# Relative-position values in one attention layer: four queries' columns side by side, all heads and batches moving, and a 32x32 block turn on VectorE

## The chip, the cores and the metric

The program runs on one core of a Trainium2 chip. The metric is the device time of one execution in microseconds (us), as the median of three runs. Lower is better. Everything said of the hardware below is read from one profiled execution of the kernel before the change.

## The reference

The program is a decoder of twelve layers over 8 batches (B) of 128 tokens with 128 channels. The change touches one of them, `l2_attn`: attention with 16 heads of 8 channels and with relative-position embeddings, both for the keys and for the values. Cut to what matters:

```
q, k, v = x @ Wq.T + bq, x @ Wk.T + bk, x @ Wv.T + bv        # (B, T, H*D), B=8, T=128, H=16, D=8
idx = clip(i - j, -128, 128) + 128                           # query i, key j
score1 = einsum('bhqd,bhkd->bhqk', qh, kh)
s2 = einsum('bhqd,qkd->qbhk', qh, rel_k_emb[idx]).reshape(T, H, B, T).transpose(2, 1, 0, 3)
attn = softmax((score1 + s2) / sqrt(D))
w1 = einsum('bhqk,bhkd->bhqd', attn, vh)
se = attn.reshape(B * H, T, T).transpose(1, 0, 2)
w2 = einsum('qnk,qkd->qnd', se, rel_v_emb[idx])              # a table of its own for every query
w2 = w2.reshape(T, H, B, D).transpose(2, 1, 0, 3)            # read back as (head, batch), not (batch, head)
out = (w1 + w2) merged over heads @ Wo.T + bo
```

The change concerns `w2`. For each of the 128 queries there is a table of 128 keys by 8 channels, and it is multiplied with that query's attention weights of all 128 pairs of batch and head. The reference flattens the pairs as (batch, head) and reads them back as (head, batch), so the result of one pair is added to the output of another.

## The kernel before, in words

`layer_l2_attn` (L2400) is one block of the program, with a barrier before and behind it. Each engine runs its own list of instructions in order and waits on semaphores. Its parts, in order of time:

- Projections, and the relative scores: 128 matmuls of L2497, one for each query.
- The attention loop, 16 steps. TensorE makes scores (L508, L2506), VectorE takes the maximum and subtracts it (L584, L590), TensorE turns them (L524), ScalarE takes the exponential into `sm.prob` (L625). `sm.prob` holds, for each of the 128 key partitions, 128 rows (one for each head and batch) of 128 queries (4 bytes each, so one query's value stands 512 bytes from the next row's). `pe_values` (L535) multiplies values with the exponentials: stationary 9 columns (8 channels and a column of ones, which gives the sum of the exponentials), moving 128 neighbouring queries, four matmuls in turn into the partitions 0, 32, 64 and 96 of bank 6. ScalarE copies that bank out (L634), `pe_back` (L543) turns it back into bank 7, and `dve_norm` takes the reciprocal of the ninth column (L597) and multiplies (L599).
- The relative values. For each query q the stationary operand is `relv[:, q, :]` (9 columns, the ninth is ones again), and the moving one is a quarter of the exponentials of that query: 32 rows of `sm.prob`, each one value. Four such matmuls fill the partitions 32i to 32i+8 of a bank, 16 queries a bank, eight rounds for the eight banks (L2539). After each round ScalarE (L2596, even rounds) or VectorE (L2639, odd rounds) copies the bank to `oR`.
- The tail, a batch at a time: four transposes from `oR` to a bank (L2549), reciprocal of the ninth column (L2647), multiplication (L2652), GpSimd adds the result to the attention output (L2462), TensorE turns the sum (L548, `pe_turn_out`), ScalarE copies it (L630, `act_outT`), TensorE projects with Wo (L553, `pe_project`), and VectorE adds it to the residual (L606, `dve_add`).

Then comes the block of `l2_xattn`, which begins with layer norm on VectorE (L421 and on), projections of the context on TensorE (L674, L677) and transposes (L453). The weights of a layer are loaded by a DMA one layer ahead. The banks are eight PSUM tensors of their own.

The two matmuls that the prediction compares, L535 and L2539:

```python
                v = self.nc.tensor.matmul(self.core.ps[6][32 * i:32 * i + 9, j * P:(j + 1) * P],
                                          self.vaug[:, b, 4 * j + i, :], self.prob_of(n)[:, i, :],
                                          start=True, stop=True)
...
                        m = nc.tensor.matmul(
                            ps[r][32 * i:32 * i + 9, 32 * t:32 * t + 32].rearrange("p (b j) -> p b j", b=B),
                            relv[:, q, :], read_by[:, i % 2, i // 2, :, :, q], start=True, stop=True)
```

Of the kernel before, what the change touches and what calls it, by code (L numbers as in the profile page):

```python
# [24 lines left out]
P = 128  # L25

B = 8
# [430 lines left out]
class SmallHeads:  # L458
# [10 lines left out]
    def __init__(self, core, c, wo, more=None, o=None):  # L469
# [9 lines left out]
        self.oT, self.inv, self.o2 = m.take(BANK), m.take(2, 16), m.take(2, P)  # L479
# [4 lines left out]

    def prob_of(self, n):

        return self.prob[:, n % 4, :, :]

# [105 lines left out]
    def dve_norm(self, dve, b, bank):  # L594
        dve.wait_ge(self.back.sem, self.back.at(b))
        o = self.core.ps[bank][:, :].rearrange("p (h d) -> p h d", d=32)
        self.nc.vector.reciprocal(self.inv[:, b % 2, :], o[:, :, 8]).then_inc(self.inverse.sem, self.inverse.up())  # L597
        dve.wait_ge(self.inverse.sem, self.inverse.at(b))
        self.nc.vector.tensor_tensor(self.o_of(b), o[:, :, 0:8],  # L599
                                     self.inv[:, b % 2, :].unsqueeze(2).broadcast_to([P, 16, 8]), ALU.mult) \  # L600
            .then_inc(self.normed.sem, self.normed.up())
# [1785 lines left out]
class RelativeHeads(SmallHeads):  # L2387
# [7 lines left out]

    def prob_of(self, n):
# [3 lines left out]
def layer_l2_attn(core, tag, w):  # L2400
# [12 lines left out]
    oR = qm.rearrange("p i t -> p (i t)").rearrange("p (b j t) -> p b j t", b=B, j=4)  # L2413
    part, part_inv = w.take(2 * 16, 8).rearrange("p (u h) d -> p u h d", u=2), w.take(2, 16)
    made_of = sm.prob.rearrange("p (b h) q -> p b h q", b=B)
    read_by = sm.prob.rearrange("p (y s m z) q -> p y z s m q", y=2, s=8, z=2)
# [11 lines left out]

    def made_in(r, n):
# [5 lines left out]
     rel_made, rel_out_act, rel_out_dve, x_biased, relv_made, relv_act, relv_dve, relv_back,  # L2435
     relv_inverse, relv_normed, relv_summed) = (
        core.count(n) for n in ("ones_set", "x_out", "queries_made", "keys_made", "values_made", "masked_out",
                                "queries_out", "keys_read", "keys_out", "values_out", "rel_made", "rel_out_act",
                                "rel_out_dve", "x_biased", "relv_made", "relv_act", "relv_dve", "relv_back",
                                "relv_inverse", "relv_normed", "relv_summed"))  # L2440
    half = lambda h: slice(h * BANK, h * BANK + BANK)
    with nc.Block(tag, no_gpsimd_drain=True) as block:

        @block.gpsimd
        def _(pool):
# [20 lines left out]
        def _(pe):  # L2466
# [43 lines left out]
            for p in range(-2, sm.STEPS + 2):  # L2510
# [11 lines left out]
                if p % 2 and p >= 3:  # L2522
                    b = (p - 3) // 2
                    pe.wait_ge(sm.outs.sem, sm.outs.at(b))
                    if b > 0:
                        pe.wait_ge(sm.normed.sem, sm.normed.at(b - 1))
                    sm.pe_back(pe, b, 7)
# [5 lines left out]
            for r in range(ROUNDS):  # L2533
                if r == 7:
                    pe.wait_ge(sm.normed.sem, sm.normed.at(B - 1))
                for t in range(TURN):
                    q = r * TURN + t
                    for i in range(4):
                        m = nc.tensor.matmul(  # L2539
                            ps[r][32 * i:32 * i + 9, 32 * t:32 * t + 32].rearrange("p (b j) -> p b j", b=B),  # L2540
                            relv[:, q, :], read_by[:, i % 2, i // 2, :, :, q], start=True, stop=True)
                m.then_inc(relv_made.sem, relv_made.up())
            for step in range(B + 2):
                if step < B:
                    if step == 0:
                        pe.wait_ge(relv_act.sem, relv_act.at(3))
                        pe.wait_ge(relv_dve.sem, relv_dve.at(3))
                    for j in range(4):
                        t = nc.tensor.transpose(ps[step][:, j * P:(j + 1) * P], oR[:, step, j, :], core.ident[:, :])  # L2549
                    t.then_inc(relv_back.sem, relv_back.up())  # L2550
                if 1 <= step <= B:
                    pe.wait_ge(relv_summed.sem, relv_summed.at(step - 1))
                    sm.pe_turn_out(pe, step - 1, step - 1)
                if step >= 2:
                    sm.pe_project(pe, step - 2, step - 2)

        @block.scalar
        def _(act):
# [35 lines left out]
            for r in range(0, ROUNDS, 2):  # L2594
                act.wait_ge(relv_made.sem, relv_made.at(r))
                nc.scalar.copy(oR[:, :, :, r * TURN:(r + 1) * TURN],  # L2596
                               ps[r][:, :].rearrange("p (t b j) -> p b j t", t=TURN, b=B)) \
                    .then_inc(relv_act.sem, relv_act.up())
# [4 lines left out]
        def _(dve):  # L2603
# [33 lines left out]
            for r in range(1, ROUNDS, 2):  # L2637
                dve.wait_ge(relv_made.sem, relv_made.at(r))
                nc.vector.tensor_copy(oR[:, :, :, r * TURN:(r + 1) * TURN],  # L2639
                                      ps[r][:, :].rearrange("p (t b j) -> p b j t", t=TURN, b=B)) \  # L2640
                    .then_inc(relv_dve.sem, relv_dve.up())
            for step in range(B + 2):
                if step < B:
                    b = step
                    dve.wait_ge(relv_back.sem, relv_back.at(b))
# [1371 lines left out]
```

## Time and profile before

| | us |
|---|---|
| median of the three runs shown | 1376.2 |
| lowest and highest of them | 1375.03, 1377.79 |
| span of the profiled execution, first to last instruction | 1375.6 |
| `l2_attn`, relative values (L2539), first start to the last copy out | 903.44 to 932.69 |
| `l2_attn`, tail, to the end of the last residual addition | 932.8 to 943.42 |

Times below are counted from the start of the span. No time of the profiled execution as a whole is given apart from its span; the span lies inside the range of the three runs, 0.6 us under their median. A matmul on float32 operands stands as two records (passes) in the trace, each with a weight load of its own; a transpose stands as one. PE is TensorE, PEld its weight loads, DVE VectorE, ACT ScalarE, POOL GpSimd. PEclk is the granted TensorE clock: 1.00 is 2.4 GHz, 0.50 is 1.2 GHz. The end of a matmul record is modelled, and matmuls overlap, so the time that one takes in a row of many is told by the distance of starts, not by its duration.

### The profile page before, as it was taken

The page shows a single profiled execution, that of the slowest core. Times are in us where ns is not written, and L with a number is a line of the kernel's source. Part 1 is how long each engine was busy: PE and PEld are TensorE (multiplying, and loading weights), DVE is VectorE, ACT ScalarE, POOL GpSimd, SP SyncE. Part 2 cuts the span into 40 slices and gives each one's busy share as a digit, 9 for nine tenths or more (in the row PEclk, how much of TensorE's full clock was granted, in tenths as well). Part 3 has the DMA queues.
Part 4 walks back from the last instruction along what each step waited for, and adds up shares of the span by engine and source line. Part 5 has one row for each costly group of instructions (what it writes and reads, how often), then busy time and mean ns, then how long its engine had stood idle before and what let it go on. Part 6 is the DMA issues. An engine that isn't in the chain of part 4 may idle for free. (4 is left out here: it accounts for less than half of the span.)

```text
span 1375.6 us, 24268 instructions
## 1 busy us (share of the span) xinstructions
PE 1217.7 (89%) x9574; PEld 879.5 (64%) x9574; DVE 701.2 (51%) x2149; ACT 534.1 (39%) x1186; POOL 441.7 (32%) x521
## 2 busy tenths in 40 slices
PE   6999898999868785998798789998989999978997
PEld 5868676788723352665466487795657775556676
DVE  5555543444478335674576466626842125754512
ACT  5534242444355432354345372213433323343232
POOL 7959320000155415672675240003000002031314
PEclk9999999999956587999899999999989998988899
DMA  5000312322091000000000000000020100000412
GB/s 163 1 4 1 142 58 75 95 62 63 21 298 42 1 1 33 1 1 0 1 1 1 9 1 1 1 4 2 1 84 31 47 16 14 1 4 1 140 48 51
DMA packets 51632, 52.42 MB, mean 38 GB/s; under 512 B 19552, under 2 KB 42336, under 8 KB 50496
## 3 DMA queue, kind: packets, MB, share of 16 engines
q1 hardware_dynamic: 50496, 48.77, 11.3%
q0 software_dynamic: 1024, 2.10, 0.7%
q8 instruction: 77, 1.26, 0.4%
q14 instruction: 35, 0.29, 0.1%
HBM read 43.65 MB, written 7.21 MB: 37 GB/s over the span
## 5 line engine op out<-in xcount | busy, mean ns | idle before, releaser
L625 ACT ACTIVATE scratch<-bank 128x512 f32<-128x512 f32 x96 | 52.4, 594 | 87.8 <-PE bank L524 87.8
L584 DVE TENSOR_REDUCE scratch<-bank 128x4 f32<-128x512 f32 x96 | 63.1, 686 | 32.7 <-PE bank L2506 19.5
L447 POOL TENSOR_TENSOR ln_rstd<-ln_ve,ln_half 128x4 f32<-128x4 f32 x28 | 28.7, 1025 | 157.7 <-DVE ln_ve L426 157.6
L2770 POOL TENSOR_TENSOR scratch<-scratch 128x16 f32<-128x16 f32 x16 | 51.7, 3230 | 50.1 <-DVE scratch L3112 50.1
L1126 ACT ACTIVATE scratch<-bank 128x512 f32<-128x512 f32 x64 | 38.2, 597 | 67.8 <-PE bank L1085 67.8
L1095 PEld LDWEIGHTS bank<-scratch 128*128 128x128 f32 x512 | 59.5, 192 | 7.2 <-issue 7.2
L1145 DVE SCALAR_TENSOR_TENSOR x_res<-bank,scratch,x_res 128x128 f32<-128x128 f32 x64 | 18.0, 344 | 88.0 <-PE bank L1095 88.0
L590 DVE TENSOR_TENSOR scratch<-bank,scratch 128x512 f32<-128x512 f32 x96 | 61.4, 681 | 0.0
L1085 PE MATMUL bank<-xnT,scratch 128*128 128x512 f32 x128 | 60.1, 615 | 0.0
L1095 PE MATMUL bank<-scratch 128*128 128x128 f32 x512 | 59.6, 275 | 0.0
L524 PEld LDWEIGHTS bank<-ident,scratch 128*128 128x128 f32 x384 | 42.5, 143 | 22.6 <-DVE scratch L590 15.9
L524 PE MATMUL bank<-ident,scratch 128*128 128x128 f32 x384 | 53.4, 282 | 3.6 <-DVE scratch L590 3.6
L508 PE MATMUL bank<-scratch 32*128 32x512 f32 x192 | 53.3, 635 | 0.8 <-issue 0.8
L2799 PE MATMUL bank<-weights,xnT 128*128 128x512 f32 x64 | 39.5, 714 | 14.5 <-DVE scratch L3082 14.2
L1903 POOL TENSOR_TENSOR x_res<-x_res,scratch 128x256 f32<-128x256 f32 x4 | 2.9, 725 | 141.8 <-ACT scratch L2048 141.8
L2462 POOL TENSOR_TENSOR weights<-weights 128x128 f32<-128x128 f32 x8 | 3.7, 457 | 131.2 <-DVE weights L2652 131.2
L3314 POOL TENSOR_TENSOR scratch<-scratch 128x1024 f32<-128x1024 f32 (+5 forms) x48 | 42.9, 894 | 3.8
L1305 PEld LDWEIGHTS bank<-scratch 128*128 128x128 f32 (+1 forms) x352 | 40.6, 187 | 3.8 <-issue 2.9
L128 PE MATMUL bank<-ident 128*128 128x512 f32 x46 | 31.7, 828 | 12.8 <-PEq L3609 8.3
L3309 POOL TENSOR_TENSOR scratch<-scratch 128x2048 f32<-128x2048 f32 x8 | 36.2, 4525 | 17.8 <-DVE weights L1616 17.3
L2975 ACT ACTIVATE scratch<-bank 128x512 f32<-128x512 f32 x32 | 19.1, 597 | 58.3 <-PE bank L2799 58.3
L1305 PE MATMUL bank<-scratch 128*128 128x128 f32 (+1 forms) x352 | 41.5, 275 | 0.0
(570 smaller groups left out, 3087.3 us busy)
## 6 DMA issues: line engine op xcount, KB each, us to landing
scratch<-conv_kernels SPq DMA_DIRECT2D x8, 1024.0 KB, 11.1
scratch<-e_l_ffn_w SPq DMA_DIRECT2D x20, 256.0 KB, 2.9
scratch<-e_l_ffn_w SPq DMA_DIRECT2D x4, 1024.0 KB, 14.5
values<-scratch SPq DMA_DIRECT2D x8, 512.0 KB, 2.6
scratch<-values SPq DMA_DIRECT2D x8, 512.0 KB, 4.3
weights<-w_l_ffn SPq DMA_DIRECT2D x1, 3698.0 KB, 11.5
scratch<-e_l_ffn_w SPq DMA_DIRECT2D x4, 768.0 KB, 9.5
weights<-w_l_attn SPq DMA_DIRECT2D x1, 2560.5 KB, 8.6
```

Source lines behind the costliest of these rows:

```text
L508: s = self.nc.tensor.matmul(self.by_head(self.core.ps[n % 4][:, :]), self.qT[rows, b * P:(b + 1) * P], self.km[rows, :, b * P:(b + 1) * P] ...
L524: t = self.nc.tensor.transpose(self.core.ps[4 + n % 2][:, i * P:(i + 1) * P], self.shift[:, n % 4, i * P:(i + 1) * P], self.core.ident[:, :])
L584: self.nc.vector.tensor_reduce(self.top[:, n % 4, :], self.by_head(self.core.ps[n % 4][:, :]), AX_X, ALU.max, negate=True).then_inc(self.t ...
L590: self.nc.vector.tensor_tensor(self.by_head(self.shift[:, n % 4, :]), self.by_head(self.core.ps[n % 4][:, :]), self.top[:, n % 4, :].unsqu ...
L625: self.nc.scalar.activation(self.prob_of(n), self.by_head(self.core.ps[4 + n % 2][:, :]), ACT.Exp, scale=scale) \
L1085: nc.tensor.matmul(ps[UP_BANKS[i]][:, :], wa[e % 2][:, i * P:(i + 1) * P], core.xnT[:, half(h)], start=True, stop=True).then_inc(up_made.s ...
L1095: mm = nc.tensor.matmul(ps[Y_BANKS[u % 3]][:, t * P:(t + 1) * P], hT[h][:, i, t * P:(t + 1) * P], wb[e % 2][:, i, :], start=(i == 0), stop ...
L1126: nc.scalar.activation(hT[u % 2][:, i, :], ps[UP_BANKS[i]][:, :], act_func) \
L1305: mm = nc.tensor.matmul(ps[Y_BANKS[j % 3]][0:n, t:t + P], hT[j % 2][:, i, t:t + n], wb[:, e, i, :], start=(i == 0), stop=(i == HC - 1))
L2770: nc.gpsimd.tensor_tensor(rn, ss, power, ALU.pow).then_inc(rooted.sem, rooted.up())
L2799: nc.tensor.matmul(ps[QK_BANKS[n]][:, :], core.xnT[:, b * P:(b + 1) * P], wqkv[d][:, n * BANK:(n + 1) * BANK], start=True, stop=True).then ...
L3314: link(tt(out, prod[:, :, 0:h], prod[:, :, h:2 * h], ALU.add))
```

## The change

The relative values are made by one matmul for each query, not four: stationary `relv[:, q, :]`, now 8 columns (no ones), and moving all 128 rows of `sm.prob` for that query. Four matmuls in turn, for the queries m, 32+m, 64+m and 96+m, go to the partitions 0, 32, 64 and 96 of the same 128 columns; 32 such groups fill the eight banks. In that layout VectorE can turn blocks of 32 partitions by 32 groups straight out of PSUM, one instruction for each of 8 sets of 16 pairs, reading at a distance of 128 columns over all banks. That leaves queries on the partitions. The sums of the exponentials are not made again: `dve_norm` now keeps the reciprocals of all batches, and they are applied by a multiplication, half of it on GpSimd and half on VectorE. GpSimd then adds as before. The copies to `oR`, the 32 transposes, and the reciprocals behind them go. The last batch's `pe_back` moves from in front of the matmuls to a place among them. The eight banks become one PSUM tensor.

```diff
@@ class SmallHeads
-        self.oT, self.inv, self.o2 = m.take(BANK), m.take(2, 16), m.take(2, P)
+        self.oT, self.inv, self.o2 = m.take(BANK), self.take_inv(m), m.take(2, P)
+    def inv_of(self, b):
+        return self.inv[:, b % self.inv.shape[1], :]
@@ def dve_norm
-        self.nc.vector.reciprocal(self.inv[:, b % 2, :], o[:, :, 8]).then_inc(self.inverse.sem, self.inverse.up())
+        self.nc.vector.reciprocal(self.inv_of(b), o[:, :, 8]).then_inc(self.inverse.sem, self.inverse.up())
@@ def layer_l2_attn
-    bq1, bv, bo, relk, relv = w.take(1), w.take(D), w.take(D), w.take(2 * P), w.take(P, 9)
+    bq1, bv, bo, relk, relv = w.take(1), w.take(D), w.take(D), w.take(2 * P), w.take(P, 8)
+    relative_out = qm.rearrange("p i t -> p (i t)").rearrange("p (b h d) -> p b h d", b=B, h=16)
+    relative_of = core.banks[:, :].rearrange("p (m h b) -> p b h m", m=32, h=16)
+    exps_of = sm.prob.rearrange("p (h b) q -> p b h q", b=B)
+    inverse_of = sm.inv.rearrange("p b h -> p (b h)").rearrange("p (h b) -> p b h", b=B)
+    BY_POOL = B // 2
+    def normalise(engine, b):
+        out = relative_out[:, b, :, 0:8]
+        return engine.tensor_tensor(out, out, inverse_of[:, b, :].unsqueeze(2).broadcast_to([P, 16, 8]), ALU.mult)
@@ gpsimd
             for b in range(B):
-                pool.wait_ge(relv_normed.sem, relv_normed.at(b))
-                nc.gpsimd.tensor_tensor(sm.o_of(b), sm.o_of(b), part[:, b % 2, :, :], ALU.add) \
+                if b < BY_POOL:
+                    pool.wait_ge(relv_turned.sem, relv_turned.at(b))
+                    normalise(nc.gpsimd, b).then_inc(relv_pool.sem, relv_pool.up())
+                    pool.wait_ge(relv_pool.sem, relv_pool.at(b))
+                else:
+                    pool.wait_ge(relv_dve.sem, relv_dve.at(b - BY_POOL))
+                nc.gpsimd.tensor_tensor(sm.o_of(b), sm.o_of(b), relative_out[:, b, :, 0:8], ALU.add) \
                     .then_inc(relv_summed.sem, relv_summed.up())
@@ tensor
-            for p in range(-2, sm.STEPS + 2):
+            for p in range(-2, sm.STEPS + 1):
-            for r in range(ROUNDS):
-                if r == 7:
+            for m in range(32):
+                if m == 24:
+                    turn_back(B - 1)
+                if m == 28:
                     pe.wait_ge(sm.normed.sem, sm.normed.at(B - 1))
-                for t in range(TURN):
-                    q = r * TURN + t
-                    for i in range(4):
-                        m = nc.tensor.matmul(
-                            ps[r][32 * i:32 * i + 9, 32 * t:32 * t + 32].rearrange("p (b j) -> p b j", b=B),
-                            relv[:, q, :], read_by[:, i % 2, i // 2, :, :, q], start=True, stop=True)
-                m.then_inc(relv_made.sem, relv_made.up())
-            for step in range(B + 2):
+                for g in range(4):
+                    q = 32 * g + m
+                    r = nc.tensor.matmul(ps[m // 4][32 * g:32 * g + 8, m % 4 * P:(m % 4 + 1) * P]
+                                         .rearrange("p (b h) -> p b h", b=B), relv[:, q, :], exps_of[:, :, :, q],
+                                         start=True, stop=True)
+            r.then_inc(relv_made.sem, relv_made.up())
+            pe.wait_ge(relv_turned.sem, relv_turned.at(B - 1))
+            for step in range(B + 1):
                 if step < B:
...
-                if 1 <= step <= B:
-                    pe.wait_ge(relv_summed.sem, relv_summed.at(step - 1))
-                    sm.pe_turn_out(pe, step - 1, step - 1)
-                if step >= 2:
-                    sm.pe_project(pe, step - 2, step - 2)
+                    pe.wait_ge(relv_summed.sem, relv_summed.at(step))
+                    sm.pe_turn_out(pe, step, step)
+                if step >= 1:
+                    sm.pe_project(pe, step - 1, step - 1)
@@ scalar
-            for r in range(0, ROUNDS, 2):
-                act.wait_ge(relv_made.sem, relv_made.at(r))
-                nc.scalar.copy(oR[:, :, :, r * TURN:(r + 1) * TURN],
...
@@ vector
-            for r in range(1, ROUNDS, 2):
-                dve.wait_ge(relv_made.sem, relv_made.at(r))
-                nc.vector.tensor_copy(oR[:, :, :, r * TURN:(r + 1) * TURN],
...
-                    nc.vector.reciprocal(part_inv[:, b % 2, :], o[:, :, 8]) \
...
+            dve.wait_ge(relv_made.sem, relv_made.at(0))
+            for b in range(B):
+                nc.vector.transpose(relative_out[:, b, :, :], relative_of[:, b, :, :]) \
+                    .then_inc(relv_turned.sem, relv_turned.up())
+            for b in range(BY_POOL, B):
+                dve.wait_ge(relv_turned.sem, relv_turned.at(b))
+                normalise(nc.vector, b).then_inc(relv_dve.sem, relv_dve.up())
+            dve.wait_ge(x_biased.sem, x_biased.at(0))
+            for b in range(B):
+                sm.dve_add(dve, b, b)
@@ def build
-        core.ps = [ctx.enter_context(nc.psum_tensor(f"bank{n}", [P, BANK], F32)) for n in range(8)]
+        core.banks = ctx.enter_context(nc.psum_tensor("bank", [P, 8 * BANK], F32))
+        core.ps = [core.banks[:, n * BANK:(n + 1) * BANK] for n in range(8)]
```

## Rows read from the trace of the kernel before

**Rows 1.** The page: span, busy time of the engines.
```profile
span 1375.6 us, 24268 instructions
PE 1217.7 (89%) x9574; PEld 879.5 (64%) x9574; DVE 701.2 (51%) x2149; ACT 534.1 (39%) x1186; POOL 441.7 (32%) x521
```
**Rows 2.** Busy time by stretch: us, then busy us of each engine, PEclk, DMA.
```profile
895.00:903.40 8.40, 7.69 (x112) 6.39 (x109) 3.68 (x8) 4.28 (x8) 0.00 (x0) 1.00 0.01 2
903.40:932.00 28.60, 28.30 (x1026) 27.83 (x1024) 3.00 (x5) 2.35 (x4) 0.00 (x0) 1.00 0.02 5
932.00:943.50 11.50, 7.95 (x56) 6.23 (x56) 7.02 (x25) 2.13 (x8) 3.65 (x8) 1.00 0.01 1
```
**Rows 3.** Timeline, 901 to 933: start, us, engine, line, tiles, count.
```profile
901.09 1.06 PE L535 MATMUL bank<-scratch 128*9 128x128 f32 x32
902.22 0.58 ACT L634 COPY xnT<-bank 128x512 f32<-128x512 f32 x1 [0.81 <-PE bank L535]
902.86 0.66 PE L543 MATMUL bank<-ident,xnT 128*128 128x128 f32 x4 [0.71 <-ACT xnT L634]
903.44 25.97 PE L2539 MATMUL bank<-scratch,weights 128*9 128x32 f32 x949
...
914.81 0.59 ACT L2596 COPY weights<-bank 128x512 f32<-128x512 f32 x1 [6.70 <-PE bank L2539]
...
924.93 0.69 DVE L2639 COPY weights<-bank 128x512 f32<-128x512 f32 x1 [5.88 <-PE bank L2539]
928.15 0.59 ACT L2596 COPY weights<-bank 128x512 f32<-128x512 f32 x1 [5.92 <-PE bank L2539]
...
932.00 0.69 DVE L2639 COPY weights<-bank 128x512 f32<-128x512 f32 x1 [6.39 <-PE bank L2539]
```
**Rows 4.** Durations min/median/max in ns, line L2539.
```profile
L2539 PEld LDWEIGHTS bank<-scratch,weights x1024: 86/136/200, 903.4 to 931.6; 128*9 128x9 f32 x171
L2539 PE MATMUL bank<-scratch,weights x1024: 214/317/404, 903.4 to 931.7; 128*9 128x32 f32 x171
```
**Rows 5.** The same of lines L535 and L774, for comparison.
```profile
L535 PEld LDWEIGHTS bank<-scratch x768: 86/91/92, 841.8 to 1215.1; 128*9 128x9 f32 x192
L535 PE MATMUL bank<-scratch x768: 272/273/279, 841.8 to 1215.2; 128*9 128x128 f32 x192
L774 PEld LDWEIGHTS bank<-weights x48: 186/192/333, 1134.5 to 1140.2; 128*128 128x128 f32 x48
```
**Rows 6.** Timeline of PE at 486: line L3623, 8 stationary columns.
```profile
485.99 1.08 PE L3623 MATMUL bank<-scratch 128*8 128x128 f32 x32
```
**Rows 7.** VectorE by line: count, busy us, mean ns, idle before.
```profile
L590 DVE TENSOR_TENSOR scratch<-bank,scratch 128x512 f32<-128x512 f32 x96 | 61.4, 681 | 0.0
L2624 DVE COPY scratch<-bank 128x512 f32<-128x512 f32 x16 | 11.1, 692 | 11.0 <-PE bank L2497 11.0
L2639 DVE COPY weights<-bank 128x512 f32<-128x512 f32 x4 | 2.8, 691 | 25.4 <-PE bank L2539 25.4
```
**Rows 8.** By line, the tail, 932.5 to 943.5.
```profile
L2462 POOL TENSOR_TENSOR weights<-weights 128x128 f32<-128x128 f32 x8 | 3.7, 457 | 131.2 <-DVE weights L2652 131.2
L2652 DVE TENSOR_TENSOR weights<-bank,weights 128x128 f32<-128x128 f32 x8 | 2.3, 292 | 0.3
L606 DVE TENSOR_TENSOR x_res<-x_res,bank 128x128 f32<-128x128 f32 x8 | 2.3, 284 | 1.9 <-PE bank L553 1.9
```
**Rows 9.** Timeline, the end of the tail.
```profile
941.92 0.33 PE L548 MATMUL bank<-ident,weights 128*128 128x128 f32 x1 [0.28 <-POOL weights L2462]
942.28 0.27 ACT L630 COPY xnT<-bank 128x128 f32<-128x128 f32 x1 [0.57 <-PE bank L548]
...
942.60 0.30 PEld L553 LDWEIGHTS bank<-weights,xnT 128*128 128x128 f32 x2 [0.32 <-ACT xnT L630]
943.13 0.29 DVE L606 TENSOR_TENSOR x_res<-x_res,bank 128x128 f32<-128x128 f32 x1 [0.33 <-PE bank L553]
```
**Rows 10.** By stretch, two other idle times of PE and what follows.
```profile
791.70:795.50 3.80, 0.00 (x0) 0.00 (x0) 3.71 (x7) 3.41 (x5) 3.78 (x3) 0.88 0.00 0
795.50:801.40 5.90, 5.86 (x27) 5.89 (x28) 2.09 (x3) 3.30 (x5) 5.90 (x4) 0.50 0.00 0
801.40:805.00 3.60, 3.60 (x34) 3.60 (x33) 2.80 (x5) 2.77 (x4) 3.60 (x3) 1.00 0.02 5
1235.80:1241.60 5.80, 5.77 (x21) 5.03 (x22) 2.02 (x4) 3.17 (x6) 1.79 (x2) 0.50 0.00 0
```

More of the change, by code:

```diff
@@ L483, in take_prob, with take_inv @@
         return c.take(4, 4, P)
+    def take_inv(self, m):
+        return m.take(2, 16)
     def prob_of(self, n):
         return self.prob[:, n % 4, :, :]
+    def inv_of(self, b):
+        return self.inv[:, b % self.inv.shape[1], :]
     def o_of(self, b):
@@ L596, in dve_norm @@
         o = self.core.ps[bank][:, :].rearrange("p (h d) -> p h d", d=32)
-        self.nc.vector.reciprocal(self.inv[:, b % 2, :], o[:, :, 8]).then_inc(self.inverse.sem, self.inverse.up())
+        self.nc.vector.reciprocal(self.inv_of(b), o[:, :, 8]).then_inc(self.inverse.sem, self.inverse.up())
         dve.wait_ge(self.inverse.sem, self.inverse.at(b))
         self.nc.vector.tensor_tensor(self.o_of(b), o[:, :, 0:8],
-                                     self.inv[:, b % 2, :].unsqueeze(2).broadcast_to([P, 16, 8]), ALU.mult) \
+                                     self.inv_of(b).unsqueeze(2).broadcast_to([P, 16, 8]), ALU.mult) \
             .then_inc(self.normed.sem, self.normed.up())
@@ L2394, in take_prob, with take_inv @@
         return c.take(16 * B, P)
+    def take_inv(self, m):
+        return m.take(B, 16)
     def prob_of(self, n):
@@ L2434, in layer_l2_attn @@
     (ones_set, x_out, queries_made, keys_made, values_made, masked_out, queries_out, keys_read, keys_out, values_out,
-     rel_made, rel_out_act, rel_out_dve, x_biased, relv_made, relv_act, relv_dve, relv_back,
-     relv_inverse, relv_normed, relv_summed) = (
+     rel_made, rel_out_act, rel_out_dve, x_biased, relv_made, relv_turned, relv_pool,
+     relv_dve, relv_summed) = (
         core.count(n) for n in ("ones_set", "x_out", "queries_made", "keys_made", "values_made", "masked_out",
                                 "queries_out", "keys_read", "keys_out", "values_out", "rel_made", "rel_out_act",
-                                "rel_out_dve", "x_biased", "relv_made", "relv_act", "relv_dve", "relv_back",
-                                "relv_inverse", "relv_normed", "relv_summed"))
+                                "rel_out_dve", "x_biased", "relv_made", "relv_turned", "relv_pool",
+                                "relv_dve", "relv_summed"))
     half = lambda h: slice(h * BANK, h * BANK + BANK)
@@ L2508, in relative, with turn_back @@
                     s.then_inc(sm.scores.sem, sm.scores.up())
-            for p in range(-2, sm.STEPS + 2):
+            def turn_back(b):
+                pe.wait_ge(sm.outs.sem, sm.outs.at(b))
+                if b > 0:
+                    pe.wait_ge(sm.normed.sem, sm.normed.at(b - 1))
+                sm.pe_back(pe, b, 7)
+            for p in range(-2, sm.STEPS + 1):
                 if p == -2:
@@ L2521, in _ @@
                     sm.pe_turn(pe, p)
[L2522 to L2527, printed above, removed]
+                if p % 2 and p >= 3 and p < sm.STEPS:
+                    turn_back((p - 3) // 2)
                 if p + 2 < sm.STEPS:
@@ L2636, in _ @@
                     sm.dve_norm(dve, (p - 4) // 2, 7)
-            for r in range(1, ROUNDS, 2):
-                dve.wait_ge(relv_made.sem, relv_made.at(r))
-                nc.vector.tensor_copy(oR[:, :, :, r * TURN:(r + 1) * TURN],
[L2640 to L2645, printed above, removed]
-                    o = ps[b][:, :].rearrange("p (h d) -> p h d", d=32)
-                    nc.vector.reciprocal(part_inv[:, b % 2, :], o[:, :, 8]) \
-                        .then_inc(relv_inverse.sem, relv_inverse.up())
-                    dve.wait_ge(relv_inverse.sem, relv_inverse.at(b))
-                    if b >= 2:
-                        dve.wait_ge(relv_summed.sem, relv_summed.at(b - 2))
-                    nc.vector.tensor_tensor(part[:, b % 2, :, :], o[:, :, 0:8],
-                                            part_inv[:, b % 2, :].unsqueeze(2).broadcast_to([P, 16, 8]), ALU.mult) \
-                        .then_inc(relv_normed.sem, relv_normed.up())
-                if step == 2:
-                    dve.wait_ge(x_biased.sem, x_biased.at(0))
-                if step >= 2:
-                    sm.dve_add(dve, step - 2, step - 2)
+            dve.wait_ge(relv_made.sem, relv_made.at(0))
[8 more added lines that the diff above has]
+                sm.dve_add(dve, b, b)
 def layer_l1_ffn(core, tag, w):
@@ L3799, in lay_weights @@
                           np.tile(g[n + "rel_k_emb"][255::-1].T, (16, 1)),
-                          np.pad(g[n + "rel_v_emb"][at], ((0, 0), (0, 0), (0, 1)), constant_values=1))
+                          g[n + "rel_v_emb"][at])
     def two_heads(a):
```

11 lines of the change are left out of this document (removed).

## The prediction

> **What bounds the kernel now.** I read the page first, then the busy time by stretch, then the timeline of the block, then the durations by line. TensorE is busy for 1217.7 of 1375.6 us [rows 1]. That says little: an average over twelve layers, and matmul ends are modelled. What counts is the stretch. From 903.4 to 932.0 TensorE is busy for 28.30 of 28.60 us at clock 1.00, the others for 3.00 us at most [rows 2], and both copying engines wait for it before each copy [rows 3]. So the relative values are bound by TensorE, and each us saved there moves the barrier at the block's end. In the tail no engine is full: PE 7.95, DVE 7.02 of 11.5 us [rows 2]. It is a chain through four engines, a batch at a time.
>
> The question is what a pass of L2539 waits for. There are 1024 of them between 903.44 and about 931.9 [rows 3, 4], 27.8 ns each. The change makes 256 passes of 128 columns out of 1024 of 32: a quarter of the instructions, the same number of moving values. If a pass costs by the instruction, three quarters of the stretch go. If it costs by the value read, nearly nothing goes.
>
> The durations speak for the values. A pass of L535 has the same stationary form and four times the columns, and takes 272/273/279 ns, its weight load 86/91/92 [rows 5]. A pass of L2539 takes 214/317/404 and its weight load 86/136/200 [rows 4]. The least, 214, is where a pass of 32 columns should be (273 less 96 columns at 0.8 ns, which is 4 x 25.5 ns by 128, see below, makes 196). The middle is some 100 ns above that: the passes stand in a queue inside TensorE. If issuing were the limit they would find it empty and take their least. Nor is a weight load's latency paid serially: L774 loads 128 columns in 192 ns a pass [rows 5], which is more than the distance of passes there (48 from 1134.5 to 1140.2, 121 ns). What L2539 has and L535 has not is the moving operand's layout: neighbouring columns 1 KB apart, against 4 bytes. In L535 four passes run side by side on the four column groups: 32 in 1.06 us less the last one's 0.27, 25.5 ns each [rows 3]. I read L2539 as four streams that share one reader of single values. The new matmul's columns are 4 KB and 512 bytes apart, so it reads in the same way.
>
> **The change, part by part.**
>
> 1. Start. The first matmul of L2539 waited for ScalarE's copy and for the last batch's turn (902.22 to 903.44) [rows 3]. It now follows the last L535, at 902.0. 1.4 us earlier.
>
> 2. Matmuls, M. Two bounds from the old stretch. If only moving values cost, 2 x 128 x 128 = 32,768 as before: 28.4 us. If the words of the weight loads cost as much, there were 1024 x (32 + 9) = 41,984 words in 28.4 us, 0.676 ns a word, and there are 256 x (128 + 8) = 34,816: 23.5 us. I take the middle, 26.0. The fastest old round, between the copies at 924.93 and 928.15 [rows 3], gives 3.22 us for 128 passes, or 25.8 for all, which fits.
>
> 3. The moved turn of the last batch: four records, 0.6 us [rows 3], inside the matmuls. Its wait for ScalarE's copy ended long before (902.8), and the wait at m = 28 for `dve_norm` (0.05 + 0.26 + 0.29 us) is covered by the 16 matmuls from m = 24, 3 us. Behind them stand only matmuls. Cost 0.6. Matmuls end at 902.0 + 26.0 + 0.6 + 0.25 = 928.85.
>
> 4. VectorE's eight turns, all exposed: nothing else may start, since they read all banks. No such operation is in this trace. Nearest are 128x512 operations out of PSUM, 681 to 692 ns, the strided copy L2624 among them [rows 7]. That is the lower bound, since a turn moves the same values through the same ports; a gain on it is excluded. Upper bound: a value costs twice, 512 more values at (681 - 292)/384 = 1.01 ns [rows 7, 8], 1.21 us. I take 0.69, as a turn out of PSUM is nearest to a copy: 8 x 0.69 + 0.05 = 5.55, to 934.4.
>
> 5. Gone: the exposed last copy (0.69), 32 transposes, 8 reciprocals, 8 multiplications [rows 2, 3, 8]; they are in the old end and not in the new sum. The seven other copies were hidden.
>
> 6. Normalising. GpSimd does batches 0 to 3 as they are turned, two operations of 0.46 [rows 8] and gaps, 1.05 us a batch, done at 933.8. VectorE does the others in 4 x 0.29, to 935.6, and GpSimd adds them by 936.7. TensorE starts batch 0 at 934.45.
>
> 7. New tail. A batch is turned (0.33), copied (0.27) and projected; with the hand-overs 0.68 from turn to projection, and then 0.25, which makes 0.47 a batch with two in flight. From the last turn to the end it is 941.92 to 943.42, 1.5 us [rows 9]. 7 x 0.47 + 1.5 = 4.8, to 939.2. The eighth batch would start at 937.75, after GpSimd's 936.7, which therefore costs nothing.
>
> 8. Clock. TensorE now idles for 5.6 us, 928.85 to 934.45. Elsewhere an idle time of 3.8 us is followed by 5.90 us at 0.50, and another by 5.80 us [rows 10]; before, this tail ran at 1.00 [rows 2]. So the new tail runs at 1.2 GHz: three passes of 128 columns lie in a batch's chain, one turn and two of the projection, each 0.1 us longer, which with two batches in flight is 0.15 on seven and 0.3 on the last, 1.3; and 0.4 in the next block, which begins as the clock comes back. 1.7 us, to 940.9. Bounds: 0, and 4.0 if dense work of the next block loses half of 5.8 us as well.
>
> 9. The single PSUM tensor, the shorter weight DMA (one layer ahead) and the eight slots for reciprocals: nothing, no wait depends on them.
>
> The old end is 943.42, the new 940.9: 2.5 us less. The span goes from 1375.6 to 1373.1; the span lies 0.6 under the median of 1376.2, so the median goes to **1373.7**.
>
> **Two rules of the Trainium skill.** The strided pattern is slow in rows 4 against rows 5. The Trainium skill (SBUF — State Buffer, "Door 1: The DMA port swizzle", its note on cachelines) says that SBUF is fast only when at least two consecutive accesses hit one 16-byte line; values 4 KB apart never do, which speaks against this change. By it the new matmuls cost as the old do by the value, 28.4 us and not 26.0.
>
> Against that, the rate of 27.8 ns a pass in rows 3 is also near a constant. The Trainium skill (TensorE: Matmul & The Clock Gate, "Wait — 56ns, not 53.3ns?") says that the distance of starts never drops under about 25 ns, however few the columns. By it the old passes were bound by their number, and rival A follows. The trace agrees with the figure, but passes in rows 4 queue, which such a floor does not explain.
>
> **The rivals.**
>
> A. A pass costs by the instruction. Then the new passes run like those of L3623, which have 8 stationary and 128 neighbouring columns: 32 in 1.08 us less 0.27 [rows 6], 26.1 ns, or 256 x 26.1 = 6.7 us, 19.3 less. For it: L535, L3623 and L2539 all come to 25 to 28 ns. Against it: rows 4. Median 1354.4. Chance 0.25.
>
> B. In between: the four queries of a group lie 128 bytes apart, which before were in the same place of other rows, and so may be read side by side in part; M between 8 and 22, say 15: 1363. Nothing in the trace has that pattern. Chance 0.10.
>
> C. Slower: VectorE's turns. Each reads 32 values 512 bytes apart over all eight banks for each block, and must fill a block before it drains. The forecast has 2.5 us in hand, and slower by over 0.2% needs another 2.75 beyond: 5.25/8, that is a turn of 1.35 us or more. At 1.5 us: 1380.2. For it: no row for the operation, and all of it is exposed. Against it: strided reads of PSUM cost VectorE nothing in L2624. Chance 0.10.
>
> D. Likeliest, as worked out, 0.55. Its own range is 1370 to 1378: M from 23.5 to 28.4 (-2.5, +2.4), clock from 0 to 4.0 (-1.7, +2.3), turns up to 1.21 us (+4.2), not all at one end.
>
> **How the numbers follow.** About 0.2%, 2.75 us, is what a measurement here can tell from no change: the three runs span as much. Faster means under 1373.4. D falls there with 0.4 of its chance, in the band with 0.5, above with 0.1. Faster: 0.25 + 0.10 + 0.22 = 0.57. Same: 0.28. Slower: 0.10 + 0.05 = 0.15. A alone holds more than 0.2, so the range must reach it: 1353 to 1378.
>
> **What would show it.** Step 2: the distance of the new passes, 100 ns (right) or 26 (A), and durations well over 273. Step 4: a turn at 0.69. Step 8: PEclk 0.50 for some 6 us from 932 to 935 on. Step 7: no idle time of PE on GpSimd in the last batches. Wrong would be a stretch of matmuls under 20 us, or turns above 1 us.

## The result, and the profile after

| | before | after |
|---|---|---|
| median of the runs, us | 1374.51 (6 runs, 1369.88 to 1377.79) | 1364.37 (6 runs, 1359.69 to 1367.11) |
| ratio, 95% interval | | 0.9931 (0.9909 to 0.9952) |
| span of the profiled execution, us | 1375.6 | 1363.0 |
| first start of the value matmuls to the end of the block's last addition | 903.44 to 943.42 | 902.91 to 933.54 |

The change makes the kernel 10 us faster, 0.7%. The forecast was 2.5 us faster, and its range holds the result.

The page after, its first lines; they answer to [rows 1]:

```profile
span 1363.0 us, 22654 instructions
PE 1204.0 (88%) x8774; PEld 858.4 (63%) x8774; DVE 699.4 (51%) x2141; ACT 531.8 (39%) x1182; POOL 443.9 (33%) x525
```

800 passes and 800 weight loads are gone, but TensorE's busy time falls by 13.7 us only. Busy time by stretch (columns as in [rows 2]): the matmuls, the turns, the tail; then turns and tail once more, cut where the clock changes.

```profile
902.40:922.20 19.80, 19.79 (x288) 9.57 (x276) 0.85 (x3) 0.60 (x1) 0.00 (x0) 1.00 0.01 2
922.20:927.20 5.00, 0.00 (x0) 0.00 (x0) 4.93 (x9) 0.00 (x0) 3.43 (x8) 0.81 0.00 0
927.20:933.60 6.40, 5.75 (x24) 4.57 (x24) 3.60 (x12) 2.08 (x8) 1.81 (x4) 0.61 0.00 0
...
922.20:925.30 3.10, 0.00 (x0) 0.00 (x0) 3.03 (x6) 0.00 (x0) 2.08 (x5) 1.00 0.00 0
925.30:932.20 6.90, 4.83 (x20) 4.03 (x21) 4.64 (x13) 1.81 (x7) 3.16 (x8) 0.51 0.00 0
932.20:936.00 3.80, 2.99 (x13) 1.68 (x12) 2.90 (x17) 1.34 (x4) 0.96 (x2) 1.00 0.04 5
```

The timeline after, cut to the rows that answer to [rows 3] and [rows 9]:

```profile
902.03 1.06 PE L542 MATMUL bank<-scratch 128*9 128x128 f32 x32
...
902.91 13.98 PE L2563 MATMUL bank<-scratch,weights 128*8 128x128 f32 x192
...
916.82 0.66 PE L550 MATMUL bank<-ident,xnT 128*128 128x128 f32 x4
...
917.41 4.78 PE L2563 MATMUL bank<-scratch,weights 128*8 128x128 f32 x64
...
922.27 4.90 DVE L2652 STREAM_TRANSPOSE weights<-bank 128x512 f32<-128x512 f32 x8 [4.17 <-PE bank L2563]
923.07 0.43 POOL L2443 TENSOR_TENSOR weights<-weights,xnT 128x128 f32<-128x128 f32 x1 [115.19 <-DVE weights L2652]
...
927.09 1.41 DVE L2443 TENSOR_TENSOR weights<-weights,xnT 128x128 f32<-128x128 f32 x4
927.23 0.69 PE L555 MATMUL bank<-ident,weights 128*128 128x128 f32 x2 [5.04 <-DVE weights L2652]
...
933.25 0.29 DVE L613 TENSOR_TENSOR x_res<-x_res,bank 128x128 f32<-128x128 f32 x1 [0.29 <-PE bank L560]
```

And the durations of the new matmuls, as in [rows 4]:

```profile
L2563 PEld LDWEIGHTS bank<-scratch,weights x256: 85/118/128, 902.8 to 921.4; 128*8 128x8 f32 x128
L2563 PE MATMUL bank<-scratch,weights x256: 440/475/491, 902.9 to 921.7; 128*8 128x128 f32 x128
```

The reader is to see three things. The passes take 440 to 491 ns, against 272 to 279 for the same number of neighbouring columns [rows 5]: they queue for their moving values, as forecast. They start 70.1 ns apart, though, and not 101: 902.91 to 921.71, less the step of 0.99 over the turn in the middle (last start before it 916.42, next 917.41), over the 254 other steps. And from the last matmul on, the block runs nearly as it was worked out.

In all texts below, "ns a pass" is first to last start of the relative-value matmuls, less such gaps, over the steps left. "Block" is from the start of the last step of the attention values before them, the second half of the 32 passes shown as L542 (before, L535), to the end of the last addition: 901.53 to 943.42 before, 902.47 to 933.54 after, 41.9 and 31.1 us. These 10.8 us are the change. The spans differ by 12.6, since the profiled execution of after is 0.94 later at the block's start and 2.7 earlier behind its end. Nothing outside the block was changed, and the six times of the kernel before alone lie up to 7.9 us apart.

### The profile page after: what moved, and what is told of

Same layout as the page of the kernel before. It is cut to its first block and busy times, and to the rows that moved or that the text cites. A ratio compares the mean times of both kernels' runs of the same rounds, so it can differ in the third digit from the quotient of the medians.

```text
span 1363.0 us, 22654 instructions
## 1 busy us (share of the span) xinstructions
PE 1204.0 (88%) x8774; PEld 858.4 (63%) x8774; DVE 699.4 (51%) x2141; ACT 531.8 (39%) x1182; POOL 443.9 (33%) x525
## 3 DMA queue, kind: packets, MB, share of 16 engines
q0 software_dynamic: 1024, 2.10, 0.7%
## 5 line engine op out<-in xcount | busy, mean ns | idle before, releaser
L1378 ACT ACTIVATE scratch<-bank 128x512 f32<-128x512 f32 (+1 forms) x48 | 26.1, 544 | 38.2 <-PE bank L1301 37.0
```

## The experiments

The theory on record was that the moving values set the pace and that each costs the same wherever it lies (step 2, case D). The rival after the result: the values set it, but four streams hinder each other less when they lie 128 bytes apart (case B). The edits are to the changed kernel unless said. The kernel before took from 1367.65 to 1385.93 us on the chips used, 1.3% apart, so times are compared on one chip only, and mechanisms by the stretches of the traces.

**1. New passes, neighbouring columns.**

```diff
-    relv[:, q, :], exps_of[:, :, :, q],
+    relv[:, q, :], sm.prob[:, q, :].rearrange("p (b h) -> p b h", b=B),
```

> The changed kernel, but the moving operand of each relative-value matmul is one row of sm.prob, 128 neighbouring values, in place of one value from each of 128 rows (it multiplies other data, so the relative values are not the reference's). Theory R (the new matmuls are bound by reading values that lie apart): the stretch of 256 passes falls from 18.5 us to about 6.7 us, 26 ns a pass as in L3623, and the pass durations fall to 273 ns. Theory I (a pass has a price of its own, independent of where its moving values lie): it stays at 72 ns a pass, 18.5 us.

**2. Old passes, neighbouring columns** (an edit to the kernel before).

```diff
-    relv[:, q, :], read_by[:, i % 2, i // 2, :, :, q],
+    relv[:, q, :], sm.prob[:, q, 32 * i:32 * i + 32].rearrange("p (b j) -> p b j", b=B),
```

> The kernel before, but the moving operand of each of the 512 matmuls is 32 neighbouring values of one row of sm.prob (other data, so the relative values are not the reference's). Theory R for the old matmuls too: reading apart cost them most of the 27.8 ns a pass, so the 1024 passes fall from 28.4 us to well under 20 us (7 ns a pass would be the four-fold concurrency of L535). Theory N (the number of passes bound the old stretch): it stays at 25 to 28 ns a pass, 26 to 28 us, though the durations may fall to near 214 ns.

**3 and 4. The four streams closer together.** In the changed kernel the four groups read queries m, 32 + m, 64 + m and 96 + m. Here they read the same query, or four that are 4 bytes apart.

```diff
-    exps_of[:, :, :, q]
+    exps_of[:, :, :, m]            # 3: same query
+    exps_of[:, :, :, 4 * m + g]    # 4: next query
```

> The changed kernel, but the four matmuls of a group read the moving values of one and the same query m, not of the queries m, 32+m, 64+m, 96+m, which lie 128 bytes apart (other data). If the place of the four streams against each other made the new reads cheaper by the value (0.56 ns against 0.86 ns before, where the four streams read one query's place in other rows), the stretch gets slower than 18.5 us, towards 28 us. If only the number of values counts, it stays at 18.5 us; if the same address is served once for all four, it falls.

> The changed kernel, but the four matmuls of a group read the moving values of the queries 4m to 4m+3, which are neighbours within 16 bytes (other data). If a read fetches more than one value and the four streams can share it, the stretch falls well under 18.5 us; if each stream fetches on its own, it stays at 18.5 us or rises as in the run with one and the same query.

Measured, one run each, on one chip with the kernel before at 1367.65 us: 1344.84 (1), 1373.17 (2), 1374.3 (3) and 1367.75 (4). TensorE by line, the count, busy us and mean ns, then the idle time before; one row from each of the four traces in this order:

```profile
L2563 PE MATMUL bank<-scratch,weights 128*8 128x128 f32 x256 | 7.4, 273 | 0.0
```
```profile
L2539 PE MATMUL bank<-scratch,weights 128*9 128x32 f32 x1024 | 13.7, 227 | 13.0 <-issue 13.0
```
```profile
L2563 PE MATMUL bank<-scratch,weights x256: 375/658/956, 905.2 to 934.5; 128*8 128x128 f32 x128
```
```profile
L2563 PE MATMUL bank<-scratch,weights x256: 374/506/766, 901.9 to 924.9; 128*8 128x128 f32 x128
```

Run 1 shows that the layout is all that holds the new matmuls: 26.8 ns a pass and durations of 273, as in [rows 5], block 19.9 us instead of 31.1. Run 3 is 111.2 ns a pass, run 4 is 86.3, the change 70.1: with the same instructions and the same number of values read apart, the pace depends on where the four streams lie to each other. That is what case D excluded. And run 3 ties the old stretch to the new: in both the four groups read the same query (in run 3 the same addresses, in the old stretch four rows, so places a multiple of 512 bytes apart), and 111.2/4 is 27.8 ns for 32 columns, where the kernel before has 27.6.

Run 2 was the surprise. With neighbours the old passes should have become far cheaper; from first to last start they took 26.5 us, against 28.2 before (its block, 41.1 us, is 0.8 shorter; its whole time is higher than before, a single run within the spread that the kernel before has). The timeline of TensorE shows why:

```profile
905.60 1.71 PE L2539 MATMUL bank<-scratch,weights 128*9 128x32 f32 x181
909.25 1.26 PE L2539 MATMUL bank<-scratch,weights 128*9 128x32 f32 x128 [1.95 <-issue]
912.98 1.89 PE L2539 MATMUL bank<-scratch,weights 128*9 128x32 f32 x128 [2.46 <-issue]
916.71 1.89 PE L2539 MATMUL bank<-scratch,weights 128*9 128x32 f32 x128 [1.84 <-issue]
```

After a first 181, the passes come in parcels of 128, that is 256 instructions with their weight loads, each 3.45 to 3.73 us after the last. Within the parcel at 909.25, at clock 1.00, they take 1.26 us, and with 0.19 for the last pass itself (193 ns in the trace), (1.26 - 0.19)/127 = 8.4 ns from start to start; then TensorE waits, for nothing that the profile shows. In the same stretch the DMA view has one queue at work, in seven small bursts:

```profile
q8 instruction: 7, 0.11, 1.9%
```

Seven packets, 16 KB each: one for each parcel. In the trace each packet starts 1.0 to 1.2 us after a parcel begins, and the next parcel begins 1.2 to 1.6 us after the packet has ended. I read the waits as TensorE waiting for its own instructions; no run tries that by itself. Whatever the cause, a parcel in some 3.6 us is 28 ns a pass, close to the old stretch's 27.6. There the passes queue in every round of 128, so the reads set the pace; and the rounds took 3.74 us at first and 3.24 to 3.30 at the end, less than any parcel of run 2, so the second limit can't have held those. But it lay close beneath: a cheaper read alone (run 2) gains 1.7 us of the stretch, and fewer instructions alone (run 3, 29.3 us) nothing. The change moved both.

**5. The groups skewed by four queries.** Group g runs four steps behind group g - 1, so at one time the streams lie 28 queries, 112 bytes, apart.

```diff
-for m in range(32):
+for t in range(32 + 3 * 4):
...
     for g in range(4):
+        m = t - 4 * g
+        if not 0 <= m < 32:
+            continue
```

> The changed kernel with the same matmuls, but the four column groups no longer work on the same step: group g is 4g steps behind, so that the four streams read queries 28 apart, 112 bytes, and not 32 apart, 128 bytes; with 12 extra steps, at the ends, on which fewer than four groups work. Theory P (streams hinder each other when their values stand in the same place of a 128-byte line, as same query 111 ns, next query 86 ns and 32 apart 72 ns a pass suggest): 256 passes take clearly under 18.5 us, perhaps 10 us. Theory V (a value read apart costs what it costs, some 0.55 ns, whatever the others read): 18.5 us or more, for the ends.

**6. Rows in plain order.** The moving operand is `sm.prob[:, :, q]`, 512 bytes from value to value, where the changed kernel takes steps of 4 KB and 512 bytes; VectorE's read pattern undoes it.

> The changed kernel, but the 128 moving values of a query are read in the order of their rows, 512 bytes from one to the next, not 4096 bytes with a jump after 16. VectorE turns the columns from their new places. If the distance inside one stream sets the rate, the stretch of matmuls leaves 18.5 us by more than 1 us, either way; if it is only how the four streams stand to each other, it stays.

**7. Rows of 130 values instead of 128**, so 520 bytes from row to row; **10. of 129**, 516 bytes.

```diff
-    return c.take(16 * B, P)
+    return c.take(16 * B, P + 2)[:, :, 0:P]    # 7; P + 1 in 10
```

> The changed kernel, but the rows of sm.prob are 130 values long, not 128, so that a stream does not stay in one place of a 128-byte line: with each row it moves by 8 bytes. Theory P: the reads spread and the 256 passes take well under 18.5 us, at best 6.7 us. Theory V: 18.5 us. The attention loop, which reads and writes whole rows, keeps its time in both.

> The changed kernel with rows of 129 values, so that a stream moves by 4 bytes with each row (by 32 bytes with each step of its inner loop, eight rows). Two values more gave 55.4 ns a pass against 70.1. If the spread over a line of some size is what counts, this differs from 55.4: nearer to 26.8 ns if the streams now meet less, nearer to 70 if rows that start off an 8-byte boundary cost. If any shift does, it is 55 again.

**9. All four passes on one column group**, one after the other.

```diff
-    ps[m // 4][32 * g:32 * g + 8, ...]
+    ps[m // 4][0:8, ...]
```

> The changed kernel, but all four matmuls of a group write the partitions 0 to 7, so that they stand on one column group and run one behind the other (three quarters of the relative values are overwritten). If a value read apart costs a lone stream nothing beyond the array's own 0.83 ns, a pass takes 107 to 112 ns and the 256 passes 27 to 29 us. If each stream has its own delay for each value, as 288 ns for a pass of 128 columns in the changed kernel could mean, the passes take 288 ns each, 74 us.

One row from each trace, in the order 5, 6, 7, 10, 9, with durations and first and last start:

```profile
L2566 PE MATMUL bank<-scratch,weights x256: 374/393/400, 903.6 to 923.2; 128*8 128x128 f32 x128
```
```profile
L2563 PE MATMUL bank<-scratch,weights x256: 440/475/491, 904.2 to 923.0; 128*8 128x128 f32 x128
```
```profile
L2563 PE MATMUL bank<-scratch,weights x256: 377/404/423, 902.1 to 917.2; 128*8 128x128 f32 x128
```
```profile
L2563 PE MATMUL bank<-scratch,weights x256: 389/412/420, 903.2 to 918.5; 128*8 128x128 f32 x128
```
```profile
L2563 PE MATMUL bank<-scratch,weights x256: 374/393/397, 895.6 to 951.5; 128*8 128x128 f32 x128
```

| run | how it reads | ns a pass | result, us | kernel before on that chip |
|---|---|---|---|---|
| 1 | neighbours | 26.8 | 1344.84 | 1367.65 (1 run) |
| 9 | apart, one group | 216.6 | 1404.24 | 1379.6 (1 run) |
| 5 | apart, 112 bytes between streams | 73.5, middle 54.3 | 1375.32 | 1385.42 (10 runs) |
| 7 | apart, 520-byte rows | 55.4 | 1370.97 | 1385.42 |
| 10 | apart, 516-byte rows | 56.8 | 1374.42 | 1379.6 |
| change, 6 | apart, 128 bytes between streams | 70.1, 70.1 | (6) 1379.67 | 1385.42 |
| 4 | apart, 4 bytes between streams | 86.3 | 1367.75 | 1367.65 |
| 3 | apart, same place | 111.2 | 1374.3 | 1367.65 |

Run 9 is the measurement of the disputed cost by itself. One stream that nobody disturbs takes 216.6 ns a pass, 1.69 ns a value. A stream of neighbours takes four times 26.8, or 107 ns, in run 1, its weight loads included, 0.84 a value: a value read apart costs twice as much. That figure is of four streams at once, but a lone stream of neighbours shows nearly the same in the next block, 16 passes of 128 columns some 112 ns apart, here in run 12:

```profile
L684 PE MATMUL bank<-weights,ctxT_sb x16: 272/275/275, 924.3 to 926.0; 96*128 96x128 f32 x16
```

Four undisturbed streams would give 216.6/4 = 54.2 ns a pass. Run 5 reaches it while all four groups are at work: four steps, 32 passes, take 1.73 and 1.74 us, 54.3 ns a pass, in two stretches of its trace:

```profile
908.41:910.14 1.73, 1.73 (x37) 0.87 (x34) 0.00 (x0) 0.00 (x0) 0.00 (x0) 1.00 0.00 0
910.14:911.88 1.74, 1.74 (x38) 0.88 (x34) 0.00 (x0) 0.00 (x0) 0.00 (x0) 1.00 0.00 0
```

It loses this again at its two ends, where one group works alone (the last eight steps from start to start are 217 ns each, as in run 9), so the whole is no faster. Run 7 has no such ends: 55.4 ns a pass, 15.0 us from first to last start, a block of 27.3 us. Run 6 is the changed kernel's 70.1 to the digit: with row starts a multiple of 512 bytes apart, a stream's own step doesn't count. The floor of 54 belongs to reading apart; what lies above it, 1 to 3, 16, 32 or 57 ns, is the streams hindering each other.

The two largest are means of something that drifts. The stretches of run 4 in which its first 32 and its fifth 32 value matmul passes start, with their own busy time:

```profile
901.95:905.12 3.17, 3.17 (x33) 2.41 (x32) 1.00 0.00 0
913.09:915.47 2.38, 2.38 (x37) 1.15 (x32) 1.00 0.00 0
```

That is 99 and 74 ns a pass, and behind the turn it is slow again. Run 3 goes from 115 to 100 in the same way, the old stretch from 29 to 25. The change stays within 71 to 72, run 7 within 54 to 57 and run 9 at 216 to 217 over the same passes. Nothing tried here explains the drift.

**8. Two halves of the batches**, 512 passes of 64 columns; VectorE turns the first half under the matmuls of the second. **11** is run 8 with run 7's rows. **12** is run 11 with two matmuls that nobody reads while VectorE turns the second half.

```diff
+for z in range(2):
     for m in range(32):
...
-    ps[m // 4][32 * g:32 * g + 8, m % 4 * P:(m % 4 + 1) * P], relv[:, q, :], exps_of[:, :, :, q]
+    ps[4 * z + m // 8][32 * g:32 * g + 8, m % 8 * 64:(m % 8 + 1) * 64], relv[:, q, :], exps_of[:, 4 * z:4 * z + 4, :, q]
...
+    core.keep_clock(0, 2)      # 12 only, behind the wait for the first half's turns
```

> The changed kernel, but the pairs are done in two halves of 64, each for all queries into four banks, 256 matmuls of 64 columns, so that VectorE turns the first half while TensorE makes the second. If the number of values read sets the time of the matmuls, they still take 18 to 19 us (512 passes of 36 ns; the supply of instructions allows 26), four of the eight turns are hidden (2.4 us), TensorE idles 2.4 us less, and the block is about 3 us shorter than the changed kernel's, 28.5 us from the last values to the last addition against 31.1. If passes have a price of their own of more than 36 ns, the matmuls get slower than 19 us and the gain goes.

> Two halves of 64 pairs and rows of 130 values together. If the price of a value read apart is 1.69 ns for a stream (216.6 ns a pass on one column group) and the shift of rows takes away what the four streams cost each other, the matmuls take 256 x 55 = 14.2 us, still above what the supply of instructions allows for 512 passes (13 us), and four turns are hidden: from the last values to the last addition 29.5 - 4.5 = 25 us, against 31.1 in the changed kernel and 41.9 before. If the supply of instructions is the next bound, gaps before passes show and the matmuls take 16 us or more.

> The kernel with halves and rows of 130 values, with two matmuls of 512 columns into the free bank 0, which nothing reads, while TensorE waits for VectorE's last turns. If idle time is what lowers the clock, the tail stays at 2.4 GHz: the block is 1 to 1.5 us shorter than without them. If the sparse tail lowers it all the same, the clock falls a little later and nothing is gained; if the two last longer than the wait, up to 0.5 us is lost.

| run | ns a pass | block, us | median, us | ratio to before, 95% |
|---|---|---|---|---|
| 8 | 35.9 | 29.5 | 1372.64 (7 runs) | 0.9911 (0.9875 to 0.9947) |
| 11 | 28.6 | 25.7 | 1371.78 (4 runs) | 0.9899 (0.9863 to 0.9934) |
| 12 | 28.6 | 24.5 | 1365.3 (4 runs) | 0.9865 (0.9836 to 0.9894) |

Run 8 takes half of VectorE's turns from the path (2.51 of 4.90 us) and gets 1.6 us in the block. Between the last value matmul and the first turn TensorE now idles for about 2.0 us only, but the clock falls all the same, to 0.50 from 925.0 to 931.8. In run 11 it falls for twice as long, into the next block. Its last block stretches, then those of run 12:

```profile
919.90:923.20 3.30, 0.77 (x4) 0.50 (x4) 3.22 (x7) 0.37 (x2) 2.19 (x6) 1.00 0.00 0
923.20:936.90 13.70, 12.36 (x42) 9.13 (x42) 7.62 (x37) 4.38 (x12) 5.55 (x10) 0.50 0.01 1
```
```profile
913.70:916.80 3.10, 2.50 (x9) 0.97 (x7) 2.90 (x6) 0.27 (x1) 1.95 (x5) 1.00 0.00 0
916.80:922.20 5.40, 4.03 (x23) 2.75 (x22) 3.27 (x11) 1.86 (x7) 3.40 (x8) 1.00 0.00 0
```

The cost of the low clock is read where nothing else differs, in the timelines of 11 and of 12: the first matmuls of the next block, the same four instructions.

```profile
929.88 3.75 PE L681 MATMUL bank<-ctxT_sb,weights 96*128 96x512 f32 x4 [0.72 <-PEq L2458]
```
```profile
922.53 1.95 PE L681 MATMUL bank<-ctxT_sb,weights 96*128 96x512 f32 x4 [0.72 <-PEq L2458]
```

From these to the next projections (L692) it is 8.25 us in run 11 and 5.10 in run 12, and from the second half's first turn to the last addition 9.5 and 8.3. Together 4.4 us for two idle matmuls. In the timed runs 12 stands 6.5 us under 11, but the two intervals overlap, so the size of that step is not settled by the times; the traces show the place. Run 12 is the best version found: 17.4 us less in the block than the kernel before.

## Why the prediction was right, and where its size was off

The direction was right and the time lies in the stated range; the size was off, 2.5 us forecast against 10.1. That the range holds it is in part luck. It reached below 1370 only to take in case A, which did not come. The range of the likeliest case, D, 1370 to 1378, misses the 1364.4, and D's own sign of being wrong, a stretch of matmuls under 20 us, came: 19.3. What held of D is that the moving values read apart set the pace, and the rest of the block. One term carries nearly all of the miss.

- **Step 2, the matmuls: mis-sized.** Forecast 26.0 us (bounds 23.5 to 28.4), and with the moved turn and the last pass 26.85 from first start to the end. Measured 902.91 to 922.2, 19.3; the values alone, 256 passes of 70.1 ns, are 18.0. The working took a price per value from the old stretch, 0.68 to 0.86 ns, and moved it to the new one. But that price held hindrance among four streams on the same query (run 3: 0.87 ns a value); 128 bytes apart it is 0.55, and undisturbed 0.42 (run 5). Both bounds came from the same layout, so neither could see this. The block was forecast 2.9 us shorter (0.4 of the loss in step 8 was meant for the next block) and is 10.8 shorter; this term is 7.6 of the 7.9 us between.
- **Step 1, the start: right.** The first matmul starts 0.44 us after the last step of attention values begins, and 1.91 before: 1.5 earlier, forecast 1.4.
- **Step 3, the moved turn: right in its place, 0.92 us more than a plain step instead of 0.6:** 0.40 us pass from the last start before it (916.42) to its own (916.82). The wait for the last normalising was hidden.
- **Step 4, the turns: right, and somewhat cheaper.** 4.90 us for eight, 0.60 apart, forecast 5.55; the trace gives 718 ns for the first and 675 or 676 for the rest. The working had excluded a gain on 681 and took eight durations end to end, but the turns start closer than they last. They are all exposed. Case C is refuted: a turn that reads 512 bytes apart over eight banks takes no longer than the copy of that size.
- **Steps 5 and 6: right.** The normalising added no wait; GpSimd's last operation ends at 929.2, 4 us before the block's end.
- **Steps 7 and 8, the tail: right.** Forecast 4.8 and, of the 1.7, 1.3 in the block, together 6.1 from the last turn to the end; measured 927.17 to 933.54, 6.4. The clock was at 0.50 for 6.8 us, forecast some 6, and it came back at 932.2, before the next block, so the other 0.4 did not come. It fell while VectorE was still turning, at 925.3, not with the tail's first matmul.
- **Step 9: right.** No wait from it is seen.
- **Case A** (a price by the instruction, 0.25) did not come: the new passes, read apart, take 70.1 ns and not 26.1. Nor does run 1's 26.8 speak for it. A pass of 32 neighbouring columns takes 8.4 ns within a parcel of run 2, a quarter of the columns in a third of the time, so a pass has no price of its own of 26 ns. Yet the number of instructions does bound a long row of small passes, by their supply as I read run 2; that limit stood in no case.
- **Case B** is what happened, with its mechanism: 1363 forecast at M = 15, measured M = 18.0 and 1364.4. That the medians come closer than the two M is luck: the kernel before has 1374.51 over six runs, and the forecast started from 1376.2. B had 0.10. The reason given for so little was that nothing in the trace had the pattern. That is no evidence against it; B differed from D only in the one property that the change alters (where the four streams lie to each other), and deserved more.

The Trainium skill (SBUF — State Buffer, "Door 1: The DMA port swizzle", the note on cachelines) says that SBUF is fast only when consecutive accesses share a 16-byte line. The runs agree for a lone stream, 1.69 against 0.84 ns a value. It says nothing of several streams, and there lies the term that was off. The Trainium skill (TensorE: Matmul & The Clock Gate, "Wait — 56ns, not 53.3ns?") sets a floor of about 25 ns between starts. Run 2 does not agree: 8.4 ns from start to start within a parcel, on four column groups.

**Open.** What makes the streams hinder each other is not settled, nor why it drifts in runs 3 and 4. Places 112 bytes apart are free, 128 bytes cost 16 ns a pass, 4 bytes 32, the same place 57, and rows of 516 or 520 bytes take nearly all of it away. That looks like a shared unit of memory that repeats with the address, but that is a guess: same place and 128 bytes apart differ, which its plainest form doesn't explain. That TensorE waits for instructions in run 2 is read from its parcels and the DMA's packets alone.

## What to carry to other kernels

When small passes on four column groups are slow, two limits have to be looked for: the moving values read apart, and a limit by the number of instructions, whose likeliest cause is their supply. Here they lay within 2 us of each other, and only moving both gained more than that. If values must be read apart, look at where the four streams lie to each other: rows padded by one or two values took a fifth off the stretch. And a price read from one layout is a price for that layout; a forecast that moves it to another needs a case in which it changes.

## What the runs showed of the hardware

- Moving fp32 values 4 KB apart cost a lone stream 1.69 ns each (run 9), neighbours 0.84 (run 1). Four streams side by side come to a quarter of the lone price, 54 ns a pass of 128, when they lie 112 bytes apart (run 5), nearly so with rows of 516 or 520 bytes (55 to 57), and not when they lie 128, 4 or 0 bytes apart: 70, 86, 111.
- In 1024 cheap passes with their weight loads (run 2), all behind the first 181 came in parcels of 256 instructions, one in 3.45 to 3.73 us, with idle time between the parcels and one 16 KB packet of the instruction queue for each.
- Within a parcel, at clock 1.00, passes of 32 columns on four column groups started 8.4 ns apart (run 2).
- VectorE turns 128x512 fp32 in 32x32 blocks out of PSUM, its source 512 bytes apart, in 675 ns: a little less than it takes for a copy of that size (692, [rows 7]).
- After dense work, 2.0 us without a matmul and a sparse tail behind it were followed by 6.8 us at clock 0.50 (run 8) or 13.7 us (run 11). Two matmuls of 512 columns in that gap kept it at 1.00 (run 12).
